# A clear of 32 x 256 numbers on GpSimd behind each indirect DMA of a graph network, and a wait of the next one for it

## The chip, the core and the metric

The kernel runs on one core of one Trainium2 chip. That core has five instruction streams: PE (TensorE, matrix products), DVE (VectorE), ACT (ScalarE), POOL (GpSimd) and SP (SyncE, which here issues the ordinary DMAs). Times are device microseconds (us) of one execution of the whole program; lower is better. An indirect DMA is one whose addresses come from a tile of row numbers; here POOL issues all of them.

## What is computed

A graph of 6250 nodes with 128 numbers each and 100000 edges, sorted by destination, goes through four residual layers:

```python
edge_index = jnp.stack([src, dst])
x = _layernorm(x + _L0_gnn_ref(x, edge_index, ...))                 # two GCN convolutions, 128 -> 64 -> 128
x = _layernorm(x + _L1_gnn_ref(x, edge_index, ...))                 # mean over neighbours, dense, relu
x = _layernorm(x + _L2_gnn_ref(x, edge_attr_128, src, dst, ...))    # five edge layers
x = _layernorm(x + _L3_gnn_ref(x, edge_weight, ..., edge_index))    # two transformer convolutions, 4 heads
# L0: agg = segment_sum((h @ W)[src] * norm, dst)
# L2, five times: m = relu(h[src] + edge_attr); z = h + segment_sum(m, dst); two dense steps with batch norm; h = z + h
# L3, twice: alpha = <q[dst], k[src] + e> / sqrt(C); w = softmax of alpha over the edges of one dst;
#            out = segment_sum((v[src] + e) * w, dst) + x @ Ws + bs
```

What all ten convolutions share is a gather `h[src]` of rows of a node table that lies in DRAM, and a sum of what was gathered over the edges of each destination.

## The kernel before, in words

The program is a chain of stages, each an `nc.Block()` in which all five engines run a stream of their own and meet at a barrier at the end. Within a stage the engines wait for each other through counting semaphores, which the code calls gates: `gate.sem` is the semaphore, `gate.at(n)` the count to wait for, `gate.passed(n)` books what a stage added. `_hold` (L238) is a wait whose count may be worked out from a loop's register; then it also adds one to a tick. The order of instructions on each engine is written out by hand.

First `_start`, `_walk` and `_lots` sort out the edges. `_walk` gathers 128 numbers for 128 partitions with 21 indirect DMAs (L448) and `_lots` with 14 (L736). A block of `_lots` (its matmuls at L812 and L819, its index tile W written at L861) has POOL gather rows of the edge attributes with `_fetch` (L1024) into shelves, 192 indirect DMAs in this block, and SP stow each shelf to the DRAM tensor `sheaf_attr`; the block ends once all is stowed. The other 192 indirect DMAs of `_fetch`, of 384 in all, are "fills", a few shelves of 8 that ride along in stages of other work: 16 in the first `_table`, then 56 behind each of two sums, and so on. In a sum they come behind the sum's own gathers.

`_mixed` is the stage of layers 0 to 2, called eight times: kind "sum" for the first three, kind "edge" for the five edge layers. POOL's `fetch` gathers one bunch of BUNCH=3 times 128 rows (L1960, 447 indirect DMAs a stage, 3576 in all) into one of DRAWS=6 places of `rings`. For each bunch ACT copies the row numbers to the tile `pick` (L1975), which it may do when PE has used up the place, and makes a one-hot selection (L1982 to L1985). PE multiplies (L2056) into `part` and DVE adds `part` to the sum (L2202). Beside it the same stage serves the sorted bulk of the edges: SP loads whole blocks (`sheaf_hots`, `sheaf_attr`), DVE and ACT prepare them, PE multiplies them into `wide` (L2091) and `lump` (L2113). Its two streams share PE, DVE and ACT, in one written order, and the product of each bunch has its place in it.

`_converse` is the stage of layer 3, called twice: POOL gathers groups of GROUP=4 times 128 rows of keys and values (L1214, 832 indirect DMAs a stage, 1664 in all) into one of RING=4 places; ACT copies the row numbers to `idx` (L1226) when DVE has joined the old content of the place; PE (L1330, L1345), DVE (L1417, L1458) and ACT compute scores and products; SP spills the values (`walk_value`).

Between these lie the dense products, the tables and the norms. In all POOL issues 21 + 14 + 384 + 3576 + 1664 = 5659 indirect DMAs.

Of the kernel before, what the change touches and what calls it, by code (L numbers as in the profile page):

```python
# [20 lines left out]
GROUP = 4  # L21
RING = 4
# [74 lines left out]
def _setup(ctx, nc):  # L97
# [60 lines left out]
    c.cols = sb("cols", [P, 64])  # L158

# [68 lines left out]
    c.whole = gate("whole")  # L228
    c.names = [0]
# [8 lines left out]
def _hold(eng, gate, n, tick=None):  # L238

    v = gate.at(n)  # L240
    eng.wait_ge(gate.sem, v)
    if tick is not None and not isinstance(v, int):
        eng.sem_inc(tick.sem, 1)

# [62 lines left out]
def _walk(c, ins, dram):  # L307
# [104 lines left out]
    with nc.psum_tensor("hidden_ps", [P, 4, 512], F32) as hidden_ps, nc.Block() as block:  # L412
# [28 lines left out]
        @block.gpsimd  # L441
        def _(e):
            tiles = c.idx[:, :, :].rearrange("p a b -> p (a b)")
            _small(c, e, c.small_pool, 1, lambda: e.tensor_copy(tiles[:, 0:KBLOCKS], edge_i))
            for k in range(KBLOCKS):
                for t, (rows, src) in enumerate(((rows_d, "dst"), (rows_s, "src"), (rows_w, "w"))):
                    out = rows[:, k, :] if src == "w" else rows[:, k, :].bitcast(I32)
                    e.indirect_dma_start(out, None, ins[src],  # L448
                                         bass.IndirectOffsetOnAxis(ap=tiles[:, k:k + 1], axis=0)
                                         ).then_inc(c.gathered[t].sem, 16)  # L450
            for t in range(3):
                c.gathered[t].passed(16 * KBLOCKS)
                e.wait_ge(c.gathered[t].sem, c.gathered[t].at(0))
# [60 lines left out]
def _lots(c, ins, dram, attr, sorted_attr):  # L514
# [196 lines left out]
    with nc.Block() as block_:  # L711
# [18 lines left out]
        def _(e):  # L730
# [3 lines left out]
            for k in range(blocks):  # L734
                for t, (to, name) in enumerate(((rows_d, "dst"), (rows_s, "src"))):
                    e.indirect_dma_start(to[:, k * P:(k + 1) * P].bitcast(I32), None, ins[name],  # L736
                                         bass.IndirectOffsetOnAxis(ap=tiles[:, k:k + 1], axis=0)
                                         ).then_inc(c.gathered[t].sem, 16)
            for t in range(2):
                c.gathered[t].passed(16 * blocks)  # L740
                e.wait_ge(c.gathered[t].sem, c.gathered[t].at(0))
# [274 lines left out]
def _fetch(c, e, first, k, shelves):  # L1016

    b, use = k % len(shelves), k // len(shelves)
    size = shelves[b].shape[1]
    if use > 0:  # L1020
        e.wait_ge(c.stowed[b].sem, c.stowed[b].at(16 * use))
    for a in range(size):
        at = first + k * size + a
        e.indirect_dma_start(shelves[b][:, a, :], None, c.attr,  # L1024
                             bass.IndirectOffsetOnAxis(ap=c.edgeS[:, at:at + 1], axis=0)).then_inc(c.fetched[b].sem, 16)

# [13 lines left out]
def _stowed(c, count, shelves):  # L1040

    for b, shelf in enumerate(shelves):
        uses = len(range(b, count, len(shelves)))
        c.fetched[b].passed(16 * shelf.shape[1] * uses)
        c.stowed[b].passed(16 * uses)
# [45 lines left out]
def _converse(c, table, query, agg, odd, score, spill, dram, x, skip, offset, spare, weights=()):  # L1091
# [65 lines left out]
    with nc.psum_tensor(c.name("part"), [P, 2, GROUP, 2 * P], F32) as part, \  # L1157
# [51 lines left out]
        def _(e):  # L1209
            with _loop(e, 0, ROUNDS) as i:  # L1210
                for g in range(RING):
                    _hold(e, c.index, i * RING + g + 1, c.tick_pool)
                    for r in range(GROUP):
                        e.indirect_dma_start(gbuf[:, g, r, :], None, table,  # L1214
                                             bass.IndirectOffsetOnAxis(ap=c.idx[:, g, r:r + 1], axis=0)
                                             ).then_inc(c.gathered[g].sem, 16)
            e.wait_ge(c.product.sem, c.product.at(GROUPS))
# [395 lines left out]
    for g in c.gathered:  # L1613
        g.passed(16 * GROUP * ROUNDS)
    for g in c.spilled:
# [169 lines left out]
def _mixed(c, kind, table, agg, width, dram, room, begin=None, attr=None, weights=(), fresh=False, fill=None):  # L1785
# [71 lines left out]
    with ExitStack() as ctx:  # L1857
# [98 lines left out]
        def _(e):  # L1956
            def fetch(i, n):
                _hold(e, c.index, q_of(i, n) + 1, c.tick_pool)
                for r in range(BUNCH):
                    e.indirect_dma_start(gbuf[:, draw(n), r, 0:width], None, table,  # L1960
                                         bass.IndirectOffsetOnAxis(ap=c.pick[:, draw(n), r:r + 1], axis=0)
                                         ).then_inc(c.drawing[draw(n)].sem, 16)
            for n in range(-LEAD, 0):
# [298 lines left out]
    c.added.passed(LOOSE * BUNCH)  # L2262
    c.near.passed(LOOSE * BUNCH)
# [750 lines left out]
```

## Time and profile before

| | |
|---|---|
| median of 3 runs | 11942.19 us (11933.62 to 11957.39) |
| profiled execution, span | 11940.9 us |
| PE busy | 7779.4 us, 65% |
| DVE busy | 5508.8 us, 46% |
| ACT busy | 4782.2 us, 40% |
| POOL busy | 5772.2 us, 48% |
| indirect DMAs of `_mixed` (L1960), busy on POOL | 2587.9 + 861.3 us |
| indirect DMAs of `_converse` (L1214), busy on POOL | 1651.9 us |

The profile is of one execution; no time beside its span is given for that execution, and the span lies 1.3 us below the median of the runs. Busy is the time in which an engine's profiled instructions were under way; instructions on registers, branches and semaphores are not in it. "Idle before" is the time in which an engine did nothing ahead of an instruction, with what released it; "issue" is said where the profile shows nothing that the engine waited for.

### The profile page before, as it was taken

How to read it: one execution, taken by the hardware profiler on the slowest of the kernel's cores; microseconds unless marked ns; L12 is line 12 of the kernel's file. 1: busy time of each engine (PE TensorE's matmuls, PEld its weight loads, DVE VectorE, ACT ScalarE, POOL GpSimd, SP SyncE). 2: the span in 40 equal slices, each digit the busy share in tenths (PEclk: the TensorE clock that was granted, in tenths of full speed). 3: DMA queues.
4: the chain of work that ended last, by engine and by line, in shares of the span. 5: the costliest groups of instructions: out<-in, count | busy, mean ns of one | idle time of the engine just before them, and what ended most of it. 6: DMA issues, size and time to landing. Idle time of an engine off the chain costs nothing. (4 is left out here: it accounts for less than half of the span.)

```text
span 11940.9 us, 256001 instructions
## 1 busy us (share of the span) xinstructions
PE 7779.4 (65%) x61807; PEld 6543.1 (55%) x61808; DVE 5508.8 (46%) x14938; ACT 4782.2 (40%) x13040; POOL 5772.2 (48%) x5856
## 2 busy tenths in 40 slices
PE   5357757767767776776777777677645555455555
PEld 3345535547746675665665667576444444344454
DVE  6545533333334444445445444444535456445447
ACT  0023323332324435444444443444445555345554
POOL 2455555554455444443443443444255555465554
PEclk6568878868878887888888888788766778667777
DMA  2235532233335544544554544455344454344453
GB/s 53 66 109 146 149 87 80 81 111 94 92 90 155 150 143 130 152 150 121 156 151 120 155 150 135 139 155 152 102 130 144 146 146 131 106 142 146 143 148 105
DMA packets 1224489, 1511.30 MB, mean 127 GB/s; under 512 B 206846, under 2 KB 806434, under 8 KB 1207895
## 3 DMA queue, kind: packets, MB, share of 16 engines
q1 hardware_dynamic: 1016374, 1055.75, 28.2%
q0 software_dynamic: 207712, 450.99, 14.9%
q8 instruction: 155, 2.54, 0.1%
q14 instruction: 248, 2.02, 0.1%
HBM read 1276.37 MB, written 229.67 MB: 126 GB/s over the span
## 5 line engine op out<-in xcount | busy, mean ns | idle before, releaser
L1960 POOL DMA_INDIRECT rings<-rows_key,pick x2682 | 2587.9, 965 | 3112.8 <-ACT pick L1975 2447.1
L2091 PE MATMUL wide<-bigDEF,bigC 128*128 128x128 bf16 (+2 forms) x32256 | 2353.5, 233 | 1289.3 <-issue 1239.5
L2091 PEld LDWEIGHTS wide<-bigDEF,bigC 128*128 128x128 bf16 x32256 | 2044.1, 110 | 1614.9 <-issue 1560.1
L1214 POOL DMA_INDIRECT bigDEF<-rows_key_value,idx x1664 | 1651.9, 993 | 1372.9 <-ACT idx L1226 742.8
L2202 DVE TENSOR_TENSOR bigDEF<-bigDEF,part 128x128 f32 (+1 forms) x3576 | 1016.7, 284 | 2643.3 <-PE part L2056 1435.5
L1975 ACT COPY pick<-pairs 128x3 int32 (+1 forms) x1192 | 222.5, 189 | 3794.2 <-PE part L2056 2957.9
L2056 PE MATMUL part<-rings 128*128 128x128 f32 (+1 forms) x7152 | 1283.6, 323 | 469.5 <-issue 231.4
L2056 PEld LDWEIGHTS part<-rings 128*128 128x128 f32 (+1 forms) x7152 | 1095.2, 213 | 565.8 <-issue 487.4
L1960 POOL DMA_INDIRECT rings<-rows_hidden,pick x894 | 861.3, 963 | 757.0 <-ACT pick L1975 535.3
L1330 PE MATMUL part<-bigB,rings 128*128 x3328 | 739.0, 390 | 730.4 <-DVE bigDEF L1417 363.6
L1982 ACT ACTIVATE rings<-iota,pairs 128x128 f32<-128x128 f32 x3576 | 1173.1, 391 | 47.8 <-remote 34.8
L1330 PEld LDWEIGHTS part<-bigB,rings 128*128 128x128 f32 x3328 | 647.1, 286 | 819.6 <-issue 818.4
L2113 PE MATMUL lump<-bigDEF,bigC 128*128 128x256 f32 x3840 | 985.3, 402 | 21.8 <-DVE bigDEF L2163 19.9
L2163 DVE TENSOR_SCALAR bigDEF<-iota,rows 128x256 f32<-128x256 f32 x2304 | 681.2, 359 | 487.4 <-remote 425.4
L2113 PEld LDWEIGHTS lump<-bigDEF,bigC 128*128 128x128 f32 x3840 | 735.1, 202 | 116.3 <-DVE bigDEF L2163 23.9
L1985 ACT ACTIVATE rings<-rings,ones 128x384 f32<-128x384 f32 x1192 | 733.2, 615 | 51.3 <-remote 12.7
L1458 DVE TENSOR_TENSOR bigDEF<-bigDEF,halves 128x136 f32 x1152 | 336.8, 292 | 720.9 <-remote 397.0
L1241 ACT ACTIVATE rings<-turned 128x512 f32<-128x512 f32 x416 | 247.5, 595 | 757.6 <-remote 476.8
L1231 ACT ACTIVATE rings<-iota,pairs 128x128 f32<-128x128 f32 x1680 | 536.1, 392 | 0.0
L2148 DVE TENSOR_TENSOR rings<-rings 128x384 f32<-128x384 f32 x745 | 414.3, 556 | 179.2 <-issue 115.0
L2091 PE MATMUL wide<-bigDEF,bigB 128*128 128x128 bf16 (+1 forms) x4608 | 380.5, 241 | 173.9 <-issue 170.0
L2113 PE MATMUL lump<-bigC 128*64 128x256 f32 x1536 | 471.4, 461 | 28.2 <-DVE bigC L2163 16.2
(424 smaller groups left out, 10607.0 us busy)
## 6 DMA issues: line engine op xcount, KB each, us to landing
bigC<-sheaf_hots SPq DMA_DIRECT2D x1152, 256.0 KB
rings<-in_attr SPq DMA_DIRECT2D x2235, 64.0 KB
bigC<-sheaf_attr SPq DMA_DIRECT2D x120, 1024.0 KB
walk_value<-bigDEF SPq DMA_DIRECT2D x416, 256.0 KB
rings<-walk_value SPq DMA_DIRECT2D x416, 256.0 KB
rings<-sheaf_steps SPq DMA_DIRECT2D x192, 256.0 KB
sheaf_hots<-bigC SPq DMA_DIRECT2D x192, 256.0 KB
bigB<-sheaf_hots SPq DMA_DIRECT2D x192, 256.0 KB
```

The lines of the kernel that those rows point to most:

```text
L1214: e.indirect_dma_start(gbuf[:, g, r, :], None, table, bass.IndirectOffsetOnAxis(ap=c.idx[:, g, r:r + 1], axis=0)).then_inc(c.gathered[g].s ...
L1231: e.activation(c.sel[:, g, r, :], c.iota[:, :], ACT.Abs, bias=c.relK[:, bass.ds(q * GROUP + r, 1)], scale=-1.0).then_inc(c.near.sem, 1)
L1330: done = e.matmul(part[:, g % 2, r, 0:D + HEADS], turn[:, g % 2, r, :], query[:, bass.ds(where[r] * (D + HEADS), D + HEADS)], start=True, ...
L1960: e.indirect_dma_start(gbuf[:, draw(n), r, 0:width], None, table, bass.IndirectOffsetOnAxis(ap=c.pick[:, draw(n), r:r + 1], axis=0)).then_ ...
L1982: e.activation(to[:, r, :], c.iota[:, :], ACT.Abs, bias=c.relL[:, bass.ds(q * BUNCH + r, 1)], scale=-1.0).then_inc(c.near.sem, 1)
L1985: e.activation(to, to, ACT.Relu, bias=c.ones[:, 0:1], scale=-1.0).then_inc(c.select.sem, 1)
L2056: last = e.matmul(part[0:width, (LEAD + n) % 2, r, :], gbuf[:, draw(n), r, 0:width], sel[:, deep(n), r, :], start=True, stop=True)
L2091: last = e.matmul(to, hot, terms, start=x < LOT and x % batch == 0 and j == 2, stop=x >= MARCH - LOT, skip_group_check=True)
L2113: last = e.matmul(lump[0:width, h, 0:SPAN], room.msg[h][:, a, :], room.marks[:, a % 8, :], start=a == 0, stop=a == LOT - 1)
L2148: e.tensor_tensor(x, x, ebuf[:, deep(n), :, :], ALU.add).then_inc(c.joined.sem, 1)
L2163: e.tensor_scalar(room.marks[:, a % 8, :], c.wide_iota[:, :], c.relS[:, bass.ds(tiles(i, h, a), 1)], None, ALU.is_equal).then_inc(c.marked ...
L2202: e.tensor_tensor(into, into, part[0:width, (LEAD + n) % 2, r, :], ALU.add).then_inc(c.added.sem, 1)
```

## The change

A tile `idle` of 32 partitions by 2 times 256 numbers (f32) is new, with two gates `paused0` and `paused1`. Wherever POOL issues an indirect DMA, it now first waits until the clear behind the last one has ended, and behind the DMA stands a `memset` of one half of `idle`, whose end is counted. What every clear writes is read by nothing. The core of the diff, cut at the two places (`_walk` and `_lots`) that read like the others:

```diff
@@ -156,6 +156,7 @@
+    c.idle = sb("idle", [32, 2, 256])
@@ -226,6 +227,7 @@
+    c.paused = [gate(f"paused{i}") for i in range(2)]
@@ -241,6 +243,11 @@
+def _pause(c, eng, which):
+    eng.memset(c.idle[:, which, :], 0.0).then_inc(c.paused[which].sem, 1)
@@ -445,9 +452,13 @@
             for k in range(KBLOCKS):
                 for t, (rows, src) in enumerate(((rows_d, "dst"), (rows_s, "src"), (rows_w, "w"))):
                     out = rows[:, k, :] if src == "w" else rows[:, k, :].bitcast(I32)
+                    e.wait_ge(c.paused[0].sem, c.paused[0].at(3 * k + t))
                     e.indirect_dma_start(out, None, ins[src],
                                          bass.IndirectOffsetOnAxis(ap=tiles[:, k:k + 1], axis=0)
                                          ).then_inc(c.gathered[t].sem, 16)
+                    _pause(c, e, 0)
+            c.paused[0].passed(3 * KBLOCKS)
+            e.wait_ge(c.paused[0].sem, c.paused[0].at(0))
             for t in range(3):
                 c.gathered[t].passed(16 * KBLOCKS)
                 e.wait_ge(c.gathered[t].sem, c.gathered[t].at(0))
@@ -1021,8 +1036,10 @@
     for a in range(size):
         at = first + k * size + a
+        e.wait_ge(c.paused[1].sem, c.paused[1].at(k * size + a))
         e.indirect_dma_start(shelves[b][:, a, :], None, c.attr,
                              bass.IndirectOffsetOnAxis(ap=c.edgeS[:, at:at + 1], axis=0)).then_inc(c.fetched[b].sem, 16)
+        _pause(c, e, 1)
 
 
 def _stow(c, e, first, count, shelves):
@@ -1042,6 +1059,7 @@
+        c.paused[1].passed(shelf.shape[1] * uses)
@@ -1211,9 +1229,11 @@
                     _hold(e, c.index, i * RING + g + 1, c.tick_pool)
                     for r in range(GROUP):
+                        _hold(e, c.paused[0], (i * RING + g) * GROUP + r, c.tick_pool)
                         e.indirect_dma_start(gbuf[:, g, r, :], None, table,
                                              bass.IndirectOffsetOnAxis(ap=c.idx[:, g, r:r + 1], axis=0)
                                              ).then_inc(c.gathered[g].sem, 16)
+                        _pause(c, e, 0)
             e.wait_ge(c.product.sem, c.product.at(GROUPS))
             e.memset(odd, 0.0)
@@ -1612,6 +1632,7 @@
+    c.paused[0].passed(GROUPS * GROUP)
@@ -1957,9 +1978,11 @@
                 _hold(e, c.index, q_of(i, n) + 1, c.tick_pool)
                 for r in range(BUNCH):
+                    _hold(e, c.paused[0], q_of(i, n) * BUNCH + r, c.tick_pool)
                     e.indirect_dma_start(gbuf[:, draw(n), r, 0:width], None, table,
                                          bass.IndirectOffsetOnAxis(ap=c.pick[:, draw(n), r:r + 1], axis=0)
                                          ).then_inc(c.drawing[draw(n)].sem, 16)
+                    _pause(c, e, 0)
             for n in range(-LEAD, 0):
                 fetch(0, n)
@@ -2260,6 +2283,7 @@
+    c.paused[0].passed(LOOSE * BUNCH)
```

The rest is the same: the instructions of PE, DVE, ACT and SP stand in the same order as before. The lines below are POOL's, from the built programs; `[waits ...]` names the semaphore.

In the loop of `_converse` on POOL, with one group of four gathers, before:

```order
L1214 DMA bigDEF<-rows_key_value,idx 128x256 [waits index]
L1214 DMA bigDEF<-rows_key_value,idx 128x256 x3
L241 REGISTER_ALU
L1214 DMA bigDEF<-rows_key_value,idx 128x256 [waits index]
L1214 DMA bigDEF<-rows_key_value,idx 128x256 x3
```

The same place on POOL with the change (L1233 is the line of the gather, L250 that of the clear, L243 that of `_hold`):

```order
L243 ISA [waits index]
L1233 DMA bigDEF<-rows_key_value,idx 128x256 [waits paused0]
L250 MEMSET idle 32x256
L243 REGISTER_ALU
L1233 DMA bigDEF<-rows_key_value,idx 128x256 [waits paused0]
L250 MEMSET idle 32x256
L243 REGISTER_ALU
L1233 DMA bigDEF<-rows_key_value,idx 128x256 [waits paused0]
L250 MEMSET idle 32x256
```

The wait for `index` has moved from the first gather of a group to an instruction of its own, and each gather has a wait, a clear and a register operation of its own.

In the gathers of `_mixed` on POOL, one bunch of three, before:

```order
L1960 DMA rings<-rows_hidden,pick 128x64 [waits index]
L1960 DMA rings<-rows_hidden,pick 128x64 x2
L1960 DMA rings<-rows_hidden,pick 128x64 [waits index]
L1960 DMA rings<-rows_hidden,pick 128x64 x2
L1960 DMA rings<-rows_hidden,pick 128x64 [waits index]
```

The same gathers on POOL with the change:

```order
L243 ISA [waits index]
L1982 DMA rings<-rows_hidden,pick 128x64 [waits paused0]
L250 MEMSET idle 32x256
L243 REGISTER_ALU
L1982 DMA rings<-rows_hidden,pick 128x64 [waits paused0]
L250 MEMSET idle 32x256
L243 REGISTER_ALU
L1982 DMA rings<-rows_hidden,pick 128x64 [waits paused0]
L250 MEMSET idle 32x256
L243 REGISTER_ALU
```

Here too nothing but the pause has come between the gathers of one bunch.

## Rows read from the trace of the kernel before

**Rows 1.** The page, part 1: busy time and share of each engine.

```profile
PE 7779.4 (65%) x61807; PEld 6543.1 (55%) x61808; DVE 5508.8 (46%) x14938; ACT 4782.2 (40%) x13040; POOL 5772.2 (48%) x5856
```

**Rows 2.** The page, part 5: the groups of indirect DMAs on POOL.

```profile
L1960 POOL DMA_INDIRECT rings<-rows_key,pick x2682 | 2587.9, 965 | 3112.8 <-ACT pick L1975 2447.1
...
L1214 POOL DMA_INDIRECT bigDEF<-rows_key_value,idx x1664 | 1651.9, 993 | 1372.9 <-ACT idx L1226 742.8
...
L1960 POOL DMA_INDIRECT rings<-rows_hidden,pick x894 | 861.3, 963 | 757.0 <-ACT pick L1975 535.3
```

**Rows 3.** The timeline of the fourth edge stage: start, length, engine, line, idle before.

```profile
4816.95 0.95 POOL L1960 DMA_INDIRECT rings<-rows_key,pick  x1 [2.30 <-ACT pick L1975]
...
4817.61 1.51 PE L2091 MATMUL wide<-bigDEF,bigC 128*128 x24
...
4820.69 0.95 POOL L1960 DMA_INDIRECT rings<-rows_key,pick  x1 [0.30 <-issue]
...
4821.94 0.94 POOL L1960 DMA_INDIRECT rings<-rows_key,pick  x1 [0.30 <-issue]
...
4822.76 0.22 PE L2091 MATMUL wide<-bigDEF,bigC 128*128 128x128 bf16 x1 [1.26 <-issue]
...
4823.19 0.94 POOL L1960 DMA_INDIRECT rings<-rows_key,pick  x1 [0.31 <-issue]
...
4824.93 0.22 PE L2091 MATMUL wide<-bigDEF,bigC 128*128 128x128 bf16 x1 [1.96 <-issue]
```

**Rows 4.** Windows (us, busy and count of each engine) there, and in a converse stage.

```profile
4808.50:4820.50 12.00, 10.95 (x104) 10.34 (x105) 7.43 (x21) 7.80 (x21) 5.66 (x6) 0.87 0.51 151
4820.50:4825.50 5.00, 1.22 (x8) 0.50 (x7) 0.78 (x4) 0.82 (x2) 2.84 (x3) 0.97 0.24 68
9200.00:9216.00 16.00, 9.01 (x39) 7.30 (x37) 12.70 (x23) 7.11 (x18) 13.10 (x10) 0.50 0.39 115
```

**Rows 5.** Windows of the block at L812, columns as before.

```profile
290.00:350.00 60.00, 7.97 (x28) 6.87 (x27) 10.86 (x16) 0.47 (x2) 45.76 (x47) 0.50 0.34 104
385.00:425.00 40.00, 31.53 (x136) 27.30 (x136) 37.66 (x58) 1.68 (x7) 31.26 (x29) 0.50 0.29 88
430.00:509.00 79.00, 11.47 (x44) 10.90 (x44) 10.86 (x16) 0.47 (x2) 60.10 (x63) 0.50 0.34 103
520.00:630.00 110.00, 78.53 (x339) 68.69 (x339) 106.03 (x160) 4.70 (x20) 0.00 (x0) 0.50 0.00 1
```

**Rows 6.** Windows of whole stages: three sum, one edge, two converse.

```profile
706.00:1501.00 795.00, 549.44 (x6004) 395.46 (x6005) 388.44 (x1289) 269.04 (x760) 428.50 (x447) 0.81 0.52 144
1590.00:2401.00 811.00, 574.08 (x6029) 408.67 (x6030) 278.57 (x922) 265.25 (x762) 432.61 (x447) 0.78 0.30 81
2538.00:3378.00 840.00, 642.99 (x5987) 574.08 (x5988) 308.91 (x913) 268.27 (x754) 423.56 (x447) 0.85 0.35 101
4556.00:5429.00 873.00, 638.38 (x5976) 577.08 (x5976) 375.55 (x1054) 373.82 (x989) 433.58 (x447) 0.84 0.52 155
8580.00:10012.00 1432.00, 748.00 (x3669) 658.77 (x3670) 647.72 (x1721) 717.20 (x2115) 823.83 (x832) 0.69 0.49 144
10267.00:11692.00 1425.00, 756.44 (x3673) 670.72 (x3674) 647.41 (x1723) 716.45 (x2116) 827.26 (x832) 0.69 0.49 142
```

**Rows 7.** POOL's groups by form (two MEMSETs), and one DMA after a wait.

```profile
L1218 POOL MEMSET bigB<- 128x6800 f32 x2 | 11.5, 5764 | 10.9 <-PE part L1330 10.9
...
L297 POOL MEMSET ident<- 128x128 f32 x1 | 0.2, 204 | 0.1
...
162.60 0.97 POOL L736 DMA_INDIRECT bigC<-in_dst,idx  x1 [0.29 <-POOL idx L733]
```

**Rows 8.** The timeline at three places where a fill or the walk ends.

```profile
68.07 0.63 DVE L468 CAST bigB<-bigC 128x896 f32<-128x896 int32 x1 [31.74 <-PEq L412]
...
638.06 0.99 POOL L1024 DMA_INDIRECT bigDEF<-in_attr,W  x1 [128.58 <-ACTq L931]
...
1534.23 1.88 SPq L1035 DMA_DIRECT2D sheaf_attr<-bigDEF  x2
```

More of the change, by code:

```diff
@@ L735, in _ @@
                 for t, (to, name) in enumerate(((rows_d, "dst"), (rows_s, "src"))):
+                    e.wait_ge(c.paused[0].sem, c.paused[0].at(2 * k + t))
                     e.indirect_dma_start(to[:, k * P:(k + 1) * P].bitcast(I32), None, ins[name],
@@ L738, in _ @@
                                          ).then_inc(c.gathered[t].sem, 16)
+                    _pause(c, e, 0)
+            c.paused[0].passed(2 * blocks)
+            e.wait_ge(c.paused[0].sem, c.paused[0].at(0))
             for t in range(2):
@@ L1962, in fetch @@
                                          ).then_inc(c.drawing[draw(n)].sem, 16)
+                    _pause(c, e, 0)
             for n in range(-LEAD, 0):
```

## The prediction, made before the changed kernel ran

> **What bounds the kernel now.** I read the page's busy times first. PE, the busiest engine, works 65% of the span, POOL 48%, and no engine is near full [rows 1]. So waits decide, and since the change touches only POOL's stream, POOL's groups come next: of its 5772 us some 5101 are the indirect DMAs of the sum, edge and converse stages, at 965, 963 and 993 ns each, and the idle time ahead of them is mostly a wait for ACT's index [rows 2]. Read so, POOL is a producer with slack, for which ACT's index copy comes late, and a pause on it would cost little or nothing.
>
> The timeline says something else. In the edge stage POOL issues six indirect DMAs back to back, 0.95 us each and 0.30 us apart, so 1.25 us from start to start. During the first of them PE does a chain of 24 matmuls in 1.51 us; from the fourth on PE starts one matmul of 0.22 us and stands for one to two microseconds with "issue" as the only reason given [rows 3]. Windows put numbers on it: 104 matmuls in 12.0 us, with six DMAs in them, then 8 in 5.0 us; DVE, ACT and the other DMAs fall with PE (21 instructions, then 4; 21, then 2; 151 GB/s, then 68), and the clock does not (0.87, then 0.97) [rows 4]. It is not a wait for data, since all engines slow down in the middle of chains whose inputs are there. I call it a freeze.
>
> The block at L812 shows what a freeze goes with, since POOL streams there without waits. POOL issues 47 DMAs in 60 us and 63 in 79 us, 1.28 and 1.25 us each: PE gets 28 and 44 matmuls done, some 0.5 per us. In between 29 DMAs take 40 us, 1.38 us each: 136 matmuls, 3.4 per us. With no DMA at all PE does 339 in 110 us, 3.1 per us [rows 5]. A tenth more distance from DMA to DMA takes the freeze away, and then the DMAs cost the others nothing. In a converse stage a stretch with ten DMAs in 16 us, 1.6 us each with hardly a gap on POOL, lets PE do 39 matmuls, 2.4 per us [rows 4], where the stage's mean is 3669 in 1432 us, 2.6 per us [rows 6]. So it is dense issue that freezes the rest, not POOL being busy.
>
> How much is frozen is a reading of mine over the whole trace, not a row: of 0.7 us bins in which the four other engines start five instructions or fewer, some 200 us in each edge stage, 150 to 220 in each sum, 360 in each converse, 200 in the L812 block, about 2570 us in all. The rows give the scale: 5 of 17 us in the edge stage, 139 of 179 us of streaming in L812.
>
> **The change, part by part.** It removes nothing and adds 5659 clears, each with a wait ahead of the next DMA and, in the loops, a register operation.
>
> *One pause.* From DMA to DMA there now lie: the gap to the clear, the clear, and the release of the next DMA. The clear of 256 numbers: 128 numbers took 204 ns and 6800 took 5764 ns [rows 7], so (5764 − 204) / 6672 = 0.833 ns a number, and 204 + 128 × 0.833 = 311 ns. Fewer partitions than 128 should not matter, as each partition has its lane; no row shows it. The release: the DMA behind POOL's own copy started 0.29 us after that ended [rows 7]. The old gap of 0.30 us goes. So x = g + 0.311 + 0.29 − 0.30 = 0.30 + g, with g the gap from DMA to clear. No row has a clear behind a DMA; g lies between 0 and the 0.30 us between two DMAs, so x between 0.30 and 0.60 us. I take 0.35, near the lower end, because the long gap is one that a DMA instruction has ahead of it and plain compute need not. A loop DMA then takes 0.965 + 0.30 + 0.35 = 1.61 us, the pace of the 16 us stretch without a freeze [rows 4].
>
> *POOL as the next bound.* If freezes vanish, POOL's own stream is late next. The eight mixed stages have 3576 DMAs: 3576 × (0.9645 + 0.30 + x) = 4522 + 3576x; the converse stages 1664 × (0.9927 + 0.30 + x) = 2151 + 1664x; together 6673 + 5240x. Today those stages take 795 + 811 + 840, five times 873 (one edge stage stands for all) and 1432 + 1425, in sum 9668 us [rows 6]. POOL's floor is 8507 us at x = 0.35 (1161 less), 8245 at 0.30, 9817 at 0.60, and it meets today's time at x = 0.57.
>
> *Edge stages.* The floor is 447 × 1.615 = 722 us against 873, 151 less. Taking my 200 us of freezes from 873 leaves 673 for the chain of the others. Both are near each other and both have their waits, ACT's index and PE's order above all, so neither is met exactly: I take 778, −95 each, −475 for five.
>
> *Sum stages.* The same floor, 722, against 795, 811 and 840. The first two have less to give: the first also stores the one-hots, 144 GB/s [rows 6], the second is close to the floor already. I take −20, −40, −70: −130.
>
> *Converse.* The floor is 832 × 1.643 = 1367 us against 1432 and 1425, at most 65 less. I take half, −35 each, −70. The cover here is thin: at x = 0.45 the floor is 1450, and the stages get longer.
>
> *The L812 block.* POOL stands idle for 128.58 us before the next block's first DMA at 638.06 [rows 8], so its 192 DMAs here end at 509.5; they begin at about 236 us. Their busy time is 45.76 / 47 = 0.97 us in one window and 31.26 / 29 = 1.08 in another [rows 5]; with 1.01, 192 × (1.01 + 0.30 + 0.35) = 319 us, and they end at 555. Without freezes PE's work, 3.1 to 3.4 matmuls per us, ends before that. Then the last stores: 565 instead of 637, −70. At the slow end, x = 0.60, POOL is done at 603, still less.
>
> *What is serial.* Nothing hides POOL in the walk (21 DMAs), the block from 638 us (32), the first table's fill (8), the last 16 of the fill behind the first sum and 16 of the first norm's, whose rows SP stores only behind the shelves: 93 DMAs. In the walk DVE has idled 31.74 us for them, and behind the first sum SP's first stow at 1534.23 waits for the shelves [rows 8]. 93 × 0.35 = 33 us, and 5 for fills with little slack: +38. The lots' 14 have DVE's work beside them; the fills behind the other sums end ahead of SP's stows.
>
> Sum: −475 − 130 − 70 − 70 + 38 = −707. The profiled execution's 11940.9 us lie within 1.3 of the median, so 11942 − 707 = **11235 us**. 0.2% is 24 us, about what can be told from no change.
>
> **Rivals.**
>
> *The pause is dearer but below the crossing* (x 0.45 to 0.56). Freezes vanish, but POOL binds nearly everywhere: 9668 − 6673 − 5240x is 637 us at 0.45 and 61 at 0.56. With serial cost and L812 that gives 11300 to 11900; 11700 as one value. For it: g might be the full 0.30 us, and the register operation may add. Against: a count register op is small beside both.
>
> *A clear and DVE hold each other up.* In rows this would be DMAs and clears stretched where DVE is dense, as the L812 window with 1.38 us a DMA beside a busy DVE (31.53 us of PE's, 37.66 of DVE's 40 [rows 5]) may already show. If every clear of the loops lost 0.03 us more, 5240 × 0.03 = 157 us: 11390. The Trainium skill, page "SBUF — State Buffer", section "Who interferes with whom", says that DVE in its two-port modes and GpSimd share one pair of ports as an exclusive lock, which the longer DMAs beside a busy DVE agree with; by it a clear, which writes, is held too, and would hold DVE.
>
> *Slower: the pause at its upper price.* Place: POOL's streams in the mixed and converse stages. At x = 0.60 their floor is 9817 us, 149 more than today even with every freeze gone; with 93 × 0.6 = 56 of serial cost and −34 in L812, 12113. It decides from x = 0.56 on. For it: two waits of 0.3 us in a row are what the timeline shows between DMAs and behind a copy [rows 3, 7]. Against: x = 0.60 needs the full gap ahead of a clear.
>
> *The pause does not do what it seems to.* If the freeze comes with the total of what is queued, or with POOL instructions of any kind, spacing the DMAs by 0.35 us leaves it. The converse stages then lengthen or stay, and only the serial cost is sure: 11980, and towards 12000. For it: the distance of 1.38 against 1.28 us in L812 came together with DVE's work being dense, so cause and effect may be the other way round (the others run, and so stretch the DMAs). Against: the 16 us stretch, with POOL at 13.10 busy.
>
> **How the numbers follow.** Freezes vanish at a pause near 0.35: 0.60, likeliest, with a range of its own from 10950 to 11600. Dearer pause, still faster: 0.12. Clear and DVE: 0.05. Slower by the upper price: 0.10. No effect on freezes: 0.13, of which 0.10 slower by over 0.2% and 0.03 within. Faster 0.77, same 0.03, slower 0.20. The low end is POOL's floor, everything it allows: 11942 − 1161 + 38, about 10820, and I take 10800. The high end reaches into the no-effect case: 12000. What is left out is the upper-price case and a little at both ends, under 2 in 10.
>
> **What the profile would show.** A MEMSET idle group x5659 at about 311 ns. L1982 DMAs 1.55 to 1.65 us apart in a bunch; above 1.85 the slower rival holds. PE's matmuls of L2091 without single ones 2 us apart, and "issue" gone as what they wait for. Edge stages at 720 to 800 us with POOL over 80% taken and its wait for ACT's index mostly gone. The L812 block over by 570. The walk's end some 7 us later. If runs of single matmuls remain at 1.6 us a DMA, the freeze was not from dense issue and the forecast falls; if edge stages end near 900 with no freeze, the price of the pause was what failed.

## The result: 13157 us instead of 11950, slower by 10%

The changed kernel takes 13156.53 us in the median of 4 runs (13154.38 to 13160.31), the kernel before beside it 11949.79 (4 runs, 11933.62 to 11959.39). The ratio is 1.1012, with a 95% interval of 1.0996 to 1.1027. The forecast of 11235, and its whole range up to 12000, were wrong, and in the direction too.

**The profile after.** The busy times on top, and the groups of POOL, with the columns of [rows 1] and [rows 2]:

```profile
PE 7860.2 (60%) x61807; PEld 6750.8 (51%) x61808; DVE 5561.7 (42%) x14938; ACT 4874.7 (37%) x13040; POOL 7606.4 (58%) x11515
...
L1982 POOL DMA_INDIRECT rings<-rows_key,pick x2682 | 2602.1, 970 | 2593.5 <-POOL idle L250 1448.4
...
L1233 POOL DMA_INDIRECT bigDEF<-rows_key_value,idx x1664 | 1589.8, 955 | 1548.0 <-POOL idle L250 1154.5
...
L250 POOL MEMSET idle<- 32x256 f32 x5659 | 1856.0, 328 | 4.8
...
L1982 POOL DMA_INDIRECT rings<-rows_hidden,pick x894 | 866.4, 969 | 726.2 <-POOL idle L250 557.2
```

PE, DVE and ACT do the work they did [rows 1]. POOL has gained 1834 us of busy time, and that is the 5659 clears at 0.328 us; its DMAs cost within 4% of what they did a piece [rows 2]. What stands ahead of a DMA is another thing: 1448 us of idle time in one group and 1154 in another are now a wait for POOL's own clear.

The timeline of POOL says why. First the walk, where the count to wait for is a constant:

```profile
60.03 0.95 POOL L456 DMA_INDIRECT bigC<-in_w,idx  x1 [0.27 <-POOL idle L250]
60.98 0.33 POOL L250 MEMSET idle<- 32x256 f32 x1
61.58 0.95 POOL L456 DMA_INDIRECT bigC<-in_dst,idx  x1 [0.27 <-POOL idle L250]
```

Then an edge stage, the second of the five, where the count comes from a loop's register:

```profile
5296.77 0.95 POOL L1982 DMA_INDIRECT rings<-rows_key,pick  x1 [0.78 <-issue]
...
5297.72 0.33 POOL L250 MEMSET idle<- 32x256 f32 x1
...
5298.83 1.03 POOL L1982 DMA_INDIRECT rings<-rows_key,pick  x1 [0.78 <-POOL idle L250]
...
5299.86 0.33 POOL L250 MEMSET idle<- 32x256 f32 x1
...
5300.97 0.95 POOL L1982 DMA_INDIRECT rings<-rows_key,pick  x1 [0.78 <-POOL idle L250]
...
5301.92 0.33 POOL L250 MEMSET idle<- 32x256 f32 x1
```

In both the clear starts at the very end of the DMA (gap 0) and takes 0.33 us. In the walk the next DMA starts 0.27 us behind it, 1.55 us after the last. In the edge stage it starts 0.78 us behind it, so that from DMA to DMA there are 2.06 us (5296.77 to 5298.83) instead of the 1.25 of [rows 3]. 2.06 is also the median over the loops of `_mixed`, and 2.09 that over `_converse`.

Windows: two stretches of the L812 block, an edge stage, a converse stage.

```profile
250.00:440.00 190.00, 140.72 (x608) 123.62 (x608) 184.29 (x268) 7.78 (x33) 156.91 (x202) 0.50 0.23 71
520.00:580.00 60.00, 0.00 (x0) 0.00 (x0) 0.00 (x0) 0.00 (x0) 47.39 (x76) 0.50 0.28 84
4903.00:5839.00 936.00, 634.44 (x6130) 589.09 (x6130) 383.50 (x1072) 387.73 (x998) 579.65 (x893) 0.82 0.49 147
9155.00:10909.00 1754.00, 846.12 (x3703) 765.41 (x3703) 663.28 (x1736) 742.89 (x2131) 1064.12 (x1662) 0.64 0.40 118
```

The edge stage is 936 us long where one took 873 [rows 6], and 447 DMAs at 2.06 are 921; the converse stage is 1754 long where one took 1432 [rows 6], and 832 × 2.09 are 1739. Over the trace all eight sum and edge stages are 932 to 938 us from the start of their first DMA to the end of the last, and both converse stages some 1756: whatever their own work, they have POOL's length. In the block at L812 PE does 608 matmuls in 190 us with the DMAs running, 3.2 per us. In the stretch from 520 us it does nothing because it is through: its last product there ends at 485 us, where it was 637 before. PE's waits:

```profile
PE part L2079 <- DVE bigDEF L2225: 728.3, 128, 7.4
PE part L2079 <- DMA rings<-rows_hidden,pick: 628.8, 245, 17.6
...
PE wide L2114 <- issue: 205.8, 173, 4.6
```

"issue" ahead of `wide` was 1295 to 1409 us in profiles of the kernel before and is 206 here; ahead of the weight loads of `wide` (PEld) it was 1661 to 1770 us and is 835. PE now waits for what POOL brings late: for gathered rows, and for DVE, which waits for them.

### The profile page after: what moved, and what is told of

The parts are those of the page before. It is cut to its first block and busy times, and to the rows that moved or that the text cites. A ratio compares the mean times of both kernels' runs of the same rounds, so it can differ in the third digit from the quotient of the medians.

```text
span 13158.4 us, 271972 instructions
## 1 busy us (share of the span) xinstructions
PE 7860.2 (60%) x61807; PEld 6750.8 (51%) x61808; DVE 5561.7 (42%) x14938; ACT 4874.7 (37%) x13040; POOL 7606.4 (58%) x11515
## 3 DMA queue, kind: packets, MB, share of 16 engines
q14 instruction: 255, 2.09, 0.1%
## 5 line engine op out<-in xcount | busy, mean ns | idle before, releaser
L2114 PE MATMUL wide<-bigDEF,bigC 128*128 128x128 bf16 (+2 forms) x32256 | 2185.8, 235 | 623.6 <-DVE bigC L2198 455.9
L1233 POOL DMA_INDIRECT bigDEF<-rows_key_value,idx x1664 | 1589.8, 955 | 1548.0 <-POOL idle L250 1154.5
L250 POOL MEMSET idle<- 32x256 f32 x5659 | 1856.0, 328 | 4.8
L2005 ACT ACTIVATE rings<-iota,pairs 128x128 f32<-128x128 f32 x3576 | 1172.6, 390 | 37.8 <-PE part L2079 26.6
L1350 PE MATMUL part<-bigB,rings 128*128 x3328 | 814.5, 423 | 480.3 <-DVE bigDEF L1437 410.0
L2013 ACT ACTIVATE rings<-rings 128x384 f32<-128x384 f32 x745 | 387.3, 520 | 1794.2 <-DVE rings L2171 1586.8
L1350 PEld LDWEIGHTS part<-bigB,rings 128*128 128x128 f32 x3328 | 746.1, 324 | 535.5 <-issue 532.6
L1437 DVE TENSOR_TENSOR bigDEF<-bigDEF,part 128x512 f32<-128x512 f32 x416 | 285.9, 687 | 1309.8 <-DMA bigDEF<-rows_key_value,idx 1309.8
L1365 PE MATMUL halves<-bigA,rings 128*128 128x136 f32 x1152 | 301.9, 441 | 551.3 <-DVE bigDEF L1478 540.2
L1365 PE MATMUL halves<-bigC,rings 128*128 128x136 f32 x1152 | 300.1, 439 | 551.0 <-DVE bigDEF L1478 540.1
```

Of the source, the lines that this page charges most:

```text
L250: eng.memset(c.idle[:, which, :], 0.0).then_inc(c.paused[which].sem, 1)
L1233: e.indirect_dma_start(gbuf[:, g, r, :], None, table, bass.IndirectOffsetOnAxis(ap=c.idx[:, g, r:r + 1], axis=0)).then_inc(c.gathered[g].s ...
L1350: done = e.matmul(part[:, g % 2, r, 0:D + HEADS], turn[:, g % 2, r, :], query[:, bass.ds(where[r] * (D + HEADS), D + HEADS)], start=True, ...
L1365: done = e.matmul(halves[:, half, r % 2, 0:cell], marks[:, g, r, :], msg[:, g % 2, r, :], start=True, stop=True)
L2005: e.activation(to[:, r, :], c.iota[:, :], ACT.Abs, bias=c.relL[:, bass.ds(q * BUNCH + r, 1)], scale=-1.0).then_inc(c.near.sem, 1)
L2114: last = e.matmul(to, hot, terms, start=x < LOT and x % batch == 0 and j == 2, stop=x >= MARCH - LOT, skip_group_check=True)
```

## The experiments

A ratio is always to the kernel before in the same set of runs. That matters more than usual: the kernel before itself took 11732 to 11950 us in five sets of runs and 8959.51 in one, that of e5 to e8. Those four kernels were run once more, so that every size stands beside a kernel before of 11732 us or more.

| run | clears, and where the wait stands | us a DMA in the loops | us | before | ratio (95%) |
|---|---|---|---|---|---|
| e10_changed | the changed kernel | 2.06, 2.09 | 13156 | 11751 | 1.119 (1.117 to 1.122) |
| e1_late | 256, wait ahead of the clear | 1.45 | 11216 | 11732 | 0.958 (0.954 to 0.962) |
| e11_late | the same | 1.45 | 11230 | 11751 | 0.955 (0.953 to 0.958) |
| e2_register | none; waits on registers alone | 1.25 | 11804 | 11732 | 1.004 (1.001 to 1.007) |
| e3_tiny | 16, else as changed | 1.86, 1.89 | 12100 | 11732 | 1.032 (1.029 to 1.036) |
| e4_outer | 256, outside the loops only | 1.25 | 11716 | 11732 | 0.999 (0.997 to 1.001) |
| e12_late64 | 64, late | 1.28 | 11805 | 11751 | 1.004 (1.003 to 1.006) |
| e13_late128 | 128, late | 1.34 | 11872 | 11946 | 0.995 (0.993 to 0.997) |
| e14_bunch | 256, late, one per bunch | 1.31 mean | 11897 | 11946 | 0.995 (0.994 to 0.997) |
| e15_loops256 | 256, late, loops alone | 1.45 | 11551 | 11946 | 0.968 (0.965 to 0.972) |
| e16_loops384 | 384, late, loops alone | 1.55 | 11100 | 11946 | 0.929 (0.926 to 0.931) |
| e17_loops512 | 512, late, loops alone | 1.66 | 11196 | 11908 | 0.940 (0.939 to 0.942) |
| e18_best | e16 and clears of 64 in the fetches | 1.55 | 11006 | 11908 | 0.924 (0.923 to 0.926) |
| e5_loops | 256, late, loops alone | 1.44 | 9941 | 8960 | 1.110 (1.108 to 1.112) |
| e6_late128 | as e13 | 1.34 | 9491 | 8960 | 1.059 (1.058 to 1.061) |
| e7_late64 | as e12 | 1.28 | 9208 | 8960 | 1.028 (1.027 to 1.030) |
| e8_bunch | as e14 | 1.31 mean | 9305 | 8960 | 1.039 (1.037 to 1.040) |

e9_before, the kernel before with a profile, took 11783 us in one run. The distance in the table is the median of the trace within a run of DMAs, to about 0.01 us; for the bunches it is worked out. "Late" is the wait of e1, ahead of the clear and behind the DMA.

### What makes the pause dear: e1, e2, e3, e10, e11

e1 keeps every clear and moves one line, in both loops and in `_fetch`:

```diff
                     for r in range(GROUP):
-                        _hold(e, c.paused[0], (i * RING + g) * GROUP + r, c.tick_pool)
                         e.indirect_dma_start(gbuf[:, g, r, :], None, table,
                                              ...
+                        _hold(e, c.paused[0], (i * RING + g) * GROUP + r, c.tick_pool)
                         _pause(c, e, 0)
```

> In the loops and in the fetches the same clear of 32 x 256 stands behind each DMA, but the wait for the clear before it now stands ahead of the clear and not ahead of the DMA; walk and lots as changed. Theory A (what costs is that in the loops the next DMA's wait goes against a register's value and is released only by the end of the clear, 0.78 us from there to the DMA where a constant's wait takes 0.27): this wait is for a clear long done, so POOL's distance falls from 2.06 us to 0.95 + 0.33 + 0 to 0.3 = 1.3 to 1.6 us, the sum, edge and converse stages are no longer bound by POOL at 936 and 1755 us, and the total is 11300 to 12000 us. Rival B (the clear itself, or the further register operations on POOL, hold POOL and others up): the distance stays above 1.9 us and the total above 12800. If dense issue alone makes the freezes, 1.55 us still frees most of them (below 11600); if it takes more distance than that, the total is near the 11942 of before.

Theory A held, and the total of 11216 us lies even below the range given for it. The timeline of POOL in the same kernel as e11, inside the loop of an edge stage:

```profile
5221.18 1.47 POOL L1981 DMA_INDIRECT rings<-rows_key,pick  x1 [2.47 <-ACT pick L1998]
5222.65 0.33 POOL L250 MEMSET idle<- 32x256 f32 x1
5223.14 0.95 POOL L1981 DMA_INDIRECT rings<-rows_key,pick  x1 [0.17 <-POOL idle L250]
5224.09 0.33 POOL L250 MEMSET idle<- 32x256 f32 x1
5224.58 1.58 POOL L1981 DMA_INDIRECT rings<-rows_key,pick  x1 [0.17 <-POOL idle L250]
```

Each DMA starts 0.17 us behind the clear ahead of it. It has no wait for that clear; what stands in the brackets is inferred. The wait for that clear stands behind the DMA. It is not for a clear long done, as was expected: in the trace it is released at 5223.01, 0.03 us after the clear of 5222.65 has ended, and POOL's next register operation comes at 5223.57. But all that lies beside the DMA of 5223.14 to 5224.09, and the next clear starts with no gap. From DMA to DMA the median is 1.45 us, with the same clear in it, and the total falls from 13156 to 11230 in one set of runs, by 15%. Only the place of the wait differs.

> The kernel of e1_late once more, to stand in one call with the changed kernel: the same clears, only the place of the wait differs. If before takes 8960: POOL's floor 1.45 us a DMA binds, stages 670 and 1235 us, total 9950 to 10000, 24% less than the changed kernel. If before takes 11732 or more: ratio 0.95 to 0.965 as in e1, and 14 to 15% less than the changed kernel.

> The changed kernel once more, in the same call as its neighbours. Theory A (POOL's stream at 2.06 and 2.09 us a DMA binds the sum, edge and converse stages): these stages are 936 and 1755 us long whatever the time of the kernel before, so the total is 12900 to 13160 us: ratio 1.44 to 1.47 if before takes 8960, 1.10 to 1.12 if it takes 11732 to 11950. Rival (the pauses slow the other engines by some share): the ratio stays at 1.10 either way.

The changed kernel came out as expected; that its length is fixed whatever the kernel before takes was seen only between 11751 and 11950, not at 8960. The ratio moved (1.101, 1.119) because before moved.

e2 is the kernel before with such a wait, for the index, ahead of every gather (`_hold(e, c.index, ..., c.tick_pool)` inside the loop over `r`).

> The kernel before, with no clear, and a register-valued wait for the group's index ahead of every gather in the loops instead of ahead of the first of a group (3632 further waits, all for a count that is there). Theory A: such a wait costs only from the release on, so these lie under the DMA that runs: distance 1.25 us, total within 60 us of before. Rival B (register operations and ticks on POOL cost by themselves about 0.5 us each): 3632 x 0.5 = 1800 us of POOL's time, stages of POOL-bound length as in the changed kernel, total 12500 to 13100.

The timeline of POOL in e2, within a run:

```profile
5114.32 0.95 POOL L1964 DMA_INDIRECT rings<-rows_key,pick  x1 [0.30 <-issue]
...
5115.57 0.94 POOL L1964 DMA_INDIRECT rings<-rows_key,pick  x1 [0.30 <-issue]
...
5116.82 0.95 POOL L1964 DMA_INDIRECT rings<-rows_key,pick  x1 [0.30 <-issue]
...
5118.07 0.95 POOL L1964 DMA_INDIRECT rings<-rows_key,pick  x1 [0.30 <-issue]
```

The gap stays 0.30 us, also where a further wait lies in it. 3632 more waits and ticks are worth 0.4% (72 us, where 60 had been allowed), so it is not their number that costs.

e3 is the changed kernel with `c.idle` of 32 x 2 x 16.

> The changed kernel with a clear of 32 x 16 instead of 32 x 256, all waits kept. Theory A: POOL's distance is 0.95 + 0.11 + 0.78 = 1.84 us instead of 2.06, and the POOL-bound stages shorten in proportion: 5240 x 0.22 = 1150 us less than the changed kernel, 12000 to 12100, if no freezes come back at 1.84. Rival B, in the form that the number of instructions and not their size counts: no less than 12900.

The timeline of POOL in e3, in an edge stage:

```profile
5110.81 0.95 POOL L1982 DMA_INDIRECT rings<-rows_key,pick  x1 [0.78 <-POOL idle L250]
...
5111.76 0.12 POOL L250 MEMSET idle<- 32x16 f32 x1
...
5112.66 0.95 POOL L1982 DMA_INDIRECT rings<-rows_key,pick  x1 [0.78 <-issue]
```

The clear is 0.12 us, the release 0.78 as before, 1.86 us a DMA. The total fell to 12100, the upper end of what was expected. So 0.2 us of clear are worth some 1056 us, about what a stream that binds gives (5240 × 0.2 = 1048). "issue" ahead of `wide` is 209 us in this trace, as in the changed kernel: at 1.86 us a DMA the freezes are as good as gone though the clear is short, so it does not take a long clear to end them.

### Where the clears work: e4, e15

> The clear and its constant wait only in the walk, the lots and the fetches (419 of 5659 DMAs); the loops as before. Theory A: all of the loss is in the loops, here the first 674 us are as in the changed kernel (32 us less than before at the start of the first sum), the fills behind the sums cost a few us more, total 11900 to 11960. Rival (the pauses ahead of the loops cost too): above 11990.

e4 has them ahead of the loops and in the fills, waited for as in the changed kernel. Nothing measurable: its first sum starts at 673 us, that of e2 in the same set of runs, whose first block is as before, at 674. The loss of the change is in the loops.

> e5 once more (the late-waited clears in the loops alone), where before takes 11700 to 11950 us: within 0.004 of e11's 0.955. The clears ahead of the loops and in the fills take from e11 or give to it the difference of where the first sum starts (654 us in e11, 694 in the profile of before) and of the fills, up to 40 us either way. If before takes 8960: 1.110 as in e5.

e15 leaves them out there and has them late in the loops: 0.968, and not within 0.004 of e11's 0.955. In microseconds e15 is 321 longer than e11. 44 of them lie ahead of the first sum (698 us against 654), which is near the 40 I had allowed. But 250 lie inside the ten stages, from the first DMA of each to its last (9296 against 9046 us), where the two kernels issue the same DMAs and clears. The two ran in different sets, with 11946 and 11751 us for the kernel before, 195 apart. So the difference between the two is in the main one of condition, and this pair does not say what the clears in the fetches are worth. e18, further down, says more.

### Distance, or a break in the run: e12 to e14, e16, e17, e18

e12 and e13 differ from e11 in the size of the clear alone, e14 in its number, e16 and e17 from e15 in its size. In e16, shown against the line of the changed kernel:

```diff
-    eng.memset(c.idle[:, which, :], 0.0).then_inc(c.paused[which].sem, 1)
+    eng.memset(c.idle[:, 0:384], 0.0).then_inc(c.paused[which].sem, 1)
```

> The kernel of e7_late64 once more. If before takes 8960: ratio 1.028 as in e7. If before takes 11732 or more, the question of e7 is answered that could not be where no freezes were: distance decides, and 1.28 us leaves the freezes (0.98 to 1.00), or anything between two DMAs does (0.96 or less).

> e6 once more (clears of 32 x 128, 1.34 us a DMA), where before takes 11700 to 11950 us: if the distance decides gradually, between e12's 1.004 at 1.28 us and e11's 0.955 at 1.45 us, about 0.98 to 0.995. If 1.34 is already enough, 0.95 or less. If before takes 8960: 1.059 as in e6.

> e8 once more (one clear of 32 x 256 per bunch or group, mean 1.30 to 1.32 us a DMA), where before takes 11700 to 11950 us. If the mean distance decides: 0.99 to 1.00. If breaking the run of DMAs with something else decides: 0.955 or less. If before takes 8960: 1.038 as in e8.

1.28 us does not help (1.004, at the upper edge of what was expected), 1.34 gives half a per cent, and one clear per bunch is worth no more than that (0.995 both), though it puts something else between each three DMAs. So it is the distance, and not that POOL does something else.

A count over the traces says the same. A run here is a row of DMAs of the sum and edge stages that each start within 0.9 us of the last one's end; a DMA is called frozen when the other engines start fewer than six instructions a microsecond while it is under way. Of the fifth DMAs in a run 82% were frozen before, 79% in e12, 67% in e13 and 84% in e14, but 19% in e11, 16% in e15 and 3% in e16. Where the line is drawn moves these by up to some ten points, not their order.

> The clears in the loops alone, 32 x 384: 0.95 + 0.43 + 0.17 = 1.55 us a DMA. POOL's floor is 447 x 1.56 = 697 us in the sum and edge stages and 832 x 1.56 = 1298 in the converse stages, against the 802 and 1335 that 1.45 us gives. If fewer DMAs of a run are frozen at 1.55 than at 1.45, edge stages take 720 to 780 us and the ratio is 0.92 to 0.95. If 1.45 has taken all that distance can take, the longer clear only costs: 0.96 to 0.98. If before takes 8960: 1.18 to 1.20.

Windows of e16, an edge and a converse stage:

```profile
4278.00:5050.00 772.00, 601.42 (x5976) 521.61 (x5976) 396.71 (x1052) 377.28 (x984) 636.90 (x893) 0.92 0.58 175
7925.00:9269.00 1344.00, 761.19 (x3702) 674.54 (x3702) 661.23 (x1733) 737.46 (x2131) 1195.48 (x1663) 0.69 0.52 154
```

The trace of the kernel before that comes nearest is that of the prediction, 11941 us where before took 11946 beside e16: 772 us instead of 873, 1344 instead of 1432 [rows 6], though POOL's busy time rose by 203 and 372 us. (In e9, at 11783 us, the same stages took 857 and 1384.) The ratio lies in the range expected for fewer frozen DMAs.

> As e16, with clears of 32 x 512: 0.95 + 0.54 + 0.17 = 1.66 us a DMA. POOL's floor is 447 x 1.67 = 746 us in a sum or edge stage and 832 x 1.66 = 1382 in a converse stage. If 1.55 left freezes that 1.66 takes away, edge stages end near the floor, 750 to 770, and the converse stages lie at 1385 instead of 1344: ratio 0.925 to 0.935. If POOL's floor is all that counts from here, 0.94 to 0.96.

The windows of e17, again an edge and a converse stage:

```profile
4277.00:5044.00 767.00, 581.13 (x6090) 535.75 (x6091) 415.39 (x1079) 387.21 (x998) 686.54 (x893) 0.88 0.59 178
7848.00:9275.00 1427.00, 783.01 (x3703) 691.52 (x3704) 664.21 (x1736) 734.79 (x2130) 1279.03 (x1663) 0.68 0.49 145
```

Against e16, 1.66 us makes the edge stage 5 us shorter and the converse stage 83 us longer, since it raises its floor to 832 × 1.66 = 1381. The total came out as expected for the case that POOL's floor is all that counts from here (0.94 to 0.96), though the edge stages lie where the other case had them; the converse stage is 42 us longer than expected. Of the distances tried, 1.55 us is the best for the whole.

> e16 (32 x 384 in the loops, 1.55 us a DMA) with clears of 32 x 64 in the fetches alone (1.28 us), waited for late as well; walk and lots without. In e12, which had these fetches, the first sum started at 611 us, in e16 at 707. If the two gains add up, 11000 to 11040 us beside 11100 for e16, ratio 0.920 to 0.925; if e12's early start came from its walk and lots, 0.929 as in e16.

```diff
+        e.wait_ge(c.paused[1].sem, c.paused[1].at(k * size + a))
+        _pause(c, e, 1)
```

e18 adds in `_fetch`, behind the DMA, a clear of 64 with this wait. The first sum starts at 610 us instead of 707, and the total is 94 us below e16's. The ten stages take the same in both, 8853 and 8851 us, so all of it comes ahead of the first sum. By the ratios, which allow for the two sets of runs, it is 0.0045 or some 54 us. 11006 us is the fastest kernel here that ran beside a before of over 11700.

### The set of runs in which before took 8960 us: e5 to e8, e9

> As e1_late in the loops of the sum, edge and converse stages, and as before in the walk, the lots and the fetches (no clear there). If the loops hold all of the gain and the pauses ahead of them and behind them only their serial cost (93 DMAs by 0.2 to 0.3 us, plus about 20 us that e1's fetches lose in the L812 block through 407 instead of 430 us for walk to sum), the ratio to before lies within 0.01 of e1's 0.9577. If the pause gained in the L812 block (e1 started its first sum at 655 us, e2 with the block as before at 674 us), this one is 10 to 30 us slower than e1.

> e1_late with a clear of 32 x 128: POOL's distance in a run 1.34 instead of 1.45 us. If what relieves the others is the distance between DMAs and 1.45 us is more than enough, freezes stay rare, POOL's floor falls by 5240 x 0.107 = 560 us, and the ratio is 0.92 to 0.95. If the share of frozen DMAs grows as the distance shrinks, the ratio lies between e1's 0.9577 and 1.

> e1_late with a clear of 32 x 64: distance 0.95 + 0.16 + 0.16 = 1.27 to 1.29 us, hardly more than the 1.25 of before. If the distance decides, the freezes are back and the ratio is 0.98 to 1.00. If it is that POOL executes something else between two DMAs, and not how long, the ratio is at or below e1's 0.9577.

> e1_late with one clear of 32 x 256 behind each bunch of 3 (group of 4) instead of behind each DMA: mean distance 1.25 + 0.2/3 to 1.25 + 0.2/4, 1.30 to 1.32 us. Mean distance alone would give what e6 and e7 give at 1.27 to 1.34. If the freeze comes from a run of four or more DMAs with nothing between them (in the trace of before 2 to 4% of the first three of a run are frozen, 79% of the fifth), breaking the run once per bunch is enough: ratio 0.93 to 0.96.

All four missed: each was written for a kernel before with freezes in it. e7 and e12 are the same kernel. First e12, the window of an edge stage:

```profile
4463.00:5323.00 860.00, 637.01 (x5976) 575.52 (x5976) 376.07 (x1052) 373.49 (x986) 509.53 (x893) 0.84 0.53 157
```

and its wait of PE ahead of `wide`:

```profile
PE wide L2114 <- issue: 1363.0, 1443, 4.0
```

Then e7, the window:

```profile
3572.00:4169.00 597.00, 525.18 (x5982) 492.66 (x5983) 381.46 (x1056) 376.72 (x989) 518.37 (x892) 0.95 0.77 227
```

and the wait:

```profile
PE wide L2114 <- issue: 101.8, 118, 4.0
```

The same 447 DMAs at 1.28 us, the same matmuls: 597 us against 860, and 102 us of "issue" against 1363. By the count above 8% of the fifth DMAs in a run are frozen, and 3% of those from the seventh on.

The granted clock differs too, 0.95 against 0.84, and PE is busy for 525 us instead of 637, while DVE and ACT are busy as long as before within 2%. So PE's quicker work is 112 of the 263 us at most. Whether the higher clock comes of the missing freezes or has a cause of its own, no run tells.

The edge stages of this set have POOL's length: 447 DMAs at 1.28, 1.34 and 1.44 us are 572, 599 and 644, and the stages take 596 to 599 us in e7, 625 to 627 in e6 and 670 to 673 in e5, 24 to 29 above. So in this set more distance is more time: 1.028, 1.059, 1.110 as it grows from 1.28 to 1.34 to 1.44. That the kernel before was bound in the same way there, at 1.25 us, is what these figures suggest; it was not profiled.

> The kernel before itself, once more with a profile, since it took 11732 us beside the first four runs and 8960 us beside the second four. If the freezes are what differs, this profile has, at about 8960 us, POOL's DMAs 1.25 us apart as ever, wide's matmuls waiting for 'issue' for a few hundred us at most instead of 1409, and edge stages of 600 us or less instead of 873; at 11700 to 11950 us it looks like the trace read for the prediction. If the difference is something else (the clock, slower DMAs), the 'issue' wait stays above 1000 us at whatever time.

e9 was meant to show the kernel before in that condition and met the other, so no profile of before at 8960 us exists. The runs e1 to e4 and e5 to e8 name the same chip, 12, so the condition is not tied to that number.

## Why the prediction was wrong

**The step that failed** is the price of one pause, "The release: the DMA behind POOL's own copy started 0.29 us after that ended [rows 7]". That row, and the 0.27 us of the walk that bears it out, are waits for a constant. In the loops the count is worked out from a register. In the built order the wait is printed on the DMA's line, but in the trace it is a semaphore instruction of its own, and from the end of the clear to the DMA it is 0.78 us. 5120 of the 5659 pauses are of that kind, all but 120 of the 5240 in these stages. The other terms came out near: the gap g was 0 and the clear 0.33 us. So x was 0.33 + 0.78 − 0.30 = 0.81 us and not 0.35, and not within "0.30 and 0.60" either. "Above 1.85 the slower rival holds" was the sign named for it, and the distance was 2.06.

**The row that would have told it** was in the trace of before. The DMA at 4816.95 of [rows 3] waited for this copy:

```profile
4815.98 0.19 ACT L1975 COPY pick<-pairs 128x3 int32 x1
```

It ends at 4816.17 (4815.98 + 0.19), and the DMA starts 0.78 us later. I had read the DMA's row for its idle time and not for its release, and took the bound of a cost from the nearest row that was quick, not from the one that had the same kind of wait.

**The sum, had x been right.** The formula of the prediction, 6673 + 5240x, gives 10917 us at 0.81, and these stages took 11000 in the trace, from the first DMA of each to its last. Before they took 9670 (9668 with one edge stage for all five), so that is 1330 more; the rest of the program is 112 us shorter, of which 32 lie ahead of the first sum and 74 between the stages, some 8 at each of nine places. The structure was right: POOL's stream is next, and the crossing at 0.57 decides. The rival "the pause at its upper price" named this mechanism, this place and the point from which it decides. Only its price stopped at 0.60.

**The freezes.** The prediction said that more distance from DMA to DMA takes them away, and that the others need about 1.6 us. e16 and e17 try just that, with the release hidden, in the loops alone. For these stages the forecast was 675 us less at 1.61 to 1.64 us a DMA, a ratio of 0.943; measured were 0.929 at 1.55 us and 0.940 at 1.66. By stages in e16, against the trace of the prediction: 773 to 780 us in the edge stages where 778 was forecast; 25, 57 and 89 less in the sums where 20, 40 and 70 were; 87 and 80 less in the converse stages where 35 each was. e11, with the very clears of the change, takes 11230 us, and that this is near the forecast's 11235 is luck: it is 521 us below the kernel before of its own set, where 707 was forecast.

**What dense issue explains, and what not.** "It is dense issue that freezes the rest" holds only with an addition. e7 shows the same dense issue with next to no freezes. Something in the condition of the machine must be there too; what, no run here tells. That "a tenth more distance" is enough, as I read from the L812 windows of 1.28 and 1.38 us, was wrong in the loops: 1.34 us left 67% of the fifth DMAs frozen. For L812 that leaves the last rival's reading, by which the others run and so stretch the DMAs; no run tests it there.

**The first block.** Forecast: 70 us less, with 38 more in serial fetches and walk. Measured, between the two traces: the next block's first fetch at 595 us instead of 638, 43 less with 7 lost in the walk, and the first sum 32 earlier in all. PE's last product there ends at 485 us instead of 637, so the freezes of the block did go, and POOL was late next: 192 DMAs in 344 us, 1.79 each and not 1.66. But how much that gains is not settled, for the block left as before varies as much: its next fetch comes at 605 us in e2, 626 in e9 and 638 in the trace of the prediction, and beside e2 the clears of e4 gain 1 us. With the short late clears (64) it is 542 us in e12 and 541 in e18.

**Clear and DVE holding each other up** did not show in the clears: 0.328 us on the mean over 5659 against 0.33 for one undisturbed. No wait of DVE for POOL is among the rows that matter.

## What to carry to other kernels

Price a wait by a row of the same kind: against a constant or a register, and with the same instruction behind it. A wait that is worked off beside a running DMA hides, one between a clear and the DMA that waits for it stands whole on the path, and here the difference in place alone is 1927 us. Before a pause is put on an engine, work out the distance at which its own stream becomes the bound, and compare the measured distance in the first profile with it. A cure for a disturbance that is not always there must be timed where it is absent as well.

## What the runs showed of the hardware that was not expected

The kernel before took 11732, 11751, 11908, 11946 and 11950 us in five sets of runs, and 8960 in a sixth, each within 1% in itself. The difference is larger than any that a kernel made here. By e7 and e12 most of it is time in which the streams of all engines stand while POOL issues indirect DMAs, with a part in PE's slower work at the lower clock; its cause outside the kernel is open.

A clear of 32 partitions on GpSimd costs 0.11 us and 0.84 ns a number (0.125 at 16, 0.218 at 128, 0.325 at 256, 0.432 at 384, 0.540 at 512, medians), near the 0.833 that 128 partitions gave [rows 7].

A register-valued wait of POOL takes 0.54 us from its own end to the start of the next register operation and 0.19 from there to the DMA, in the trace of the changed kernel (medians). Where a DMA of 0.95 us runs meanwhile, as in e2 and e11, none of it shows: the gaps are 0.30 and 0.17 us.
